# Pairs of tiles in the MLP passes, biases in three bfloat16 rows, and an edge attention that clears its PSUM bank two ahead

## The reference, cut to what matters

```
x = x + gnn(ln(x)) + mix(ln(x))      # two graph attention layers and an MLP; a curvature mixer
x = x + routed_ffn(ln(x))            # an MLP whose result is scaled by a weight per node
x = x + gcn(ln(x)) + transformer(ln(x))   # graph convolution; 4 layers of linear attention and MLP
x = x + experts(ln(x))               # 4 small MLPs, gated by a graph attention over 65,536 edges

# one graph attention layer: for each edge, 8 heads of 32
e = sum(q[dst] * k[src]) / sqrt(32);  m = segment_max(e, dst);  a = exp(e - m[dst])
z = segment_sum(a, dst);  agg = segment_sum(v[src] * a, dst) / z
# one MLP: 256 -> 1024 -> 256
y = act(x @ w1 + b1) @ w2 + b2
```

## Time and profile before

| | us |
|---|---|
| median of 3 runs (lowest, highest) | 8246.72 (8228.94, 8250.25) |
| the profiled execution | 8267.04 |
| its span from first to last instruction | 8265.3 |
| PE busy, share | 5754.8, 70% |
| DVE busy, share | 4931.1, 60% |
| POOL busy, share | 4726.3, 57% |
| ACT busy, share | 2389.2, 29% |
| granted TensorE clock, mean | 0.79 of full |

### The profile page before, as it was taken

One profiled execution on the slowest core, in us unless ns is written; L12 is line 12 of the kernel. 1 busy time (PEld: TensorE's weight loads), 2 busy tenths in 40 slices (PEclk: granted clock), 3 DMA queues, 4 the chain that ended last, 5 costly groups with the idle time before them and its releaser, 6 DMA issues. The chain is left out here.

```text
span 8265.3 us, 113872 instructions
## 1 busy us (share of the span) xinstructions
PE 5754.8 (70%) x30502; PEld 4427.0 (54%) x30502; DVE 4931.1 (60%) x10093; ACT 2389.2 (29%) x6859; POOL 4726.3 (57%) x4113
## 2 busy tenths in 40 slices
PE   3443588888875888888685865957868858677743
PEld 1333455555544555555464653856756747556632
DVE  9367477787765777878676165363354453411157
ACT  0243044444440444444422311211212212122211
POOL 0777577777732777777304656565565565167730
PEclk9766777777777777877797977978979979788865
DMA  2000476666633766666400122322313324222201
GB/s 36 4 1 4 116 180 174 172 175 174 171 106 99 181 173 172 178 174 174 123 5 17 29 78 53 86 73 72 95 46 93 95 52 100 57 53 46 46 4 50
DMA packets 686241, 772.10 MB, mean 93 GB/s; under 512 B 469870, under 2 KB 514659, under 8 KB 684593
## 3 DMA queue, kind: packets, MB, share of 16 engines
q0 software_dynamic: 557488, 618.01, 30.6%
q1 hardware_dynamic: 128232, 147.68, 6.2%
HBM read 720.03 MB, written 42.63 MB: 92 GB/s over the span
## 5 line engine op out<-in xcount | busy, mean ns | idle before, releaser
L1492 POOL DMA_INDIRECT arena<-kv_rows,visit_src x1664 | 2051.7, 1233 | 872.0 <-issue 473.3
L1978 POOL DMA_INDIRECT arena<-piece_rows,visit_src x832 | 1034.5, 1243 | 799.9 <-PE ps L2035 571.8
L1645 PE MATMUL ps<-arena,w 125*125 x4992 | 917.1, 350 | 53.9 <-DVE stage L1532 39.1
L1645 PEld LDWEIGHTS ps<-arena,w 125*125 125x125 bf16 x4992 | 816.6, 176 | 184.8 <-issue 155.8
L1744 ACT CAST ps<-cat 125x265 bf16 x1664 | 637.7, 383 | 931.8 <-PE ps L1684 604.5
L1684 PE MATMUL ps<-h,cat 125*125 125x265 f32 x1664 | 700.2, 545 | 218.6 <-ACT ps L1744 194.8
L724 POOL DMA_INDIRECT sorted<-arena,cat x512 | 576.8, 1127 | 477.1 <-PEq L84 276.9
L637 PE MATMUL ps<-ht,w 128*128 128x125 f32 x6400 | 834.4, 284 | 12.0 <-DVE ht L674 7.9
L603 ACT ACTIVATE h<-ps,vec 128x125 f32<-128x125 f32 x1600 | 463.2, 366 | 1251.2 <-PE ps L637 1251.0
L637 PEld LDWEIGHTS ps<-ht,w 128*128 128x128 f32 x6400 | 768.0, 196 | 61.2 <-issue 55.6
L628 PE MATMUL ps<-ident,stage 125*128 125x125 f32 x1200 | 257.8, 300 | 753.8 <-ACT stage L588 655.2
(11 more groups left out here) (558 smaller groups left out, 9690.5 us busy)
## 6 DMA issues: line engine op xcount, KB each, us to landing
w<-rel SPq DMA_DIRECT2D x104, 488.3 KB
arena<-kv_rows,visit_src POOLq DMA_INDIRECT x1664, 5.6
arena<-rel SPq DMA_DIRECT2D x34, 512.0 KB
arena<-piece_rows,visit_src POOLq DMA_INDIRECT x832
kv_rows<-h SPq DMA_DIRECT2D x50, 250.0 KB
x_kept<-arena POOLq DMA_DIRECT2D x3, 3125.0 KB
arena<-tab,visit_src POOLq DMA_INDIRECT x537
by_low<-steer POOLq DMA_INDIRECT x512, 2.1
```

Of the source, the lines that this page charges most:

```text
L1492: nc.gpsimd.indirect_dma_start(ring[k % RG][:, j, :], None, d.kv, bass.IndirectOffsetOnAxis(g.srcv[:, v:v + 1], 0)).then_inc(got[k % RG], 16)
L1645: ins = nc.tensor.matmul(psQ[n][:, j * D:(j + 1) * D], ohT[b % 4][:, e:e + P], q[:, bass.ds(at[2 * n + j], D)], start=(m == 0), stop=(m == 2))
L1978: nc.gpsimd.indirect_dma_start(self.rows[v % (self.RG * GG)], None, self.d.pieces, bass.IndirectOffsetOnAxis(g.srcv[:, v:v + 1], 0)).then_ ...
```

## The change

- **MLP passes** (`mlp`): they go through a new `pair_pass`, two tiles at a time, so that a matmul of the hidden layer has 250 moving columns; the results of both tiles share a PSUM bank. The passes of the experts stay as they are (`expert_mlp`).
- **Biases** of these passes and of the mixer's output pass: DVE splits the row once into three bfloat16 parts (`split_bias`), and PE adds it by one bfloat16 matmul over three rows.
- **Curvature mixer**: the rescale is cut off from `attend`; the order is rescale, scale_rows of the next tile, attend, keep.
- **Edge attention**: the bank two windows on is cleared, and a visit waits for the clearing of two visits before it; the rescale stands between the halves of the product; one set of weights in SBUF, doubled by batch, serves both uses; the factor lies in another bank and no longer waits for `shift` and `turn_back`; ACT makes it before the weights.
- Some weights of 32 columns move to make room.

The diff, cut to its core:

```diff
-            step(V.tensor_scalar(wn[:, 0:VC], w, 1.0, None, ALU.add))
+            step(V.tensor_scalar(wn[:, 0:VC], w, 2.0, None, ALU.add))
...
-                    if bias:
+                    if bias and hidden:
                         ins = nc.tensor.matmul(ps[u], g.ones[0:1, 0:P], home.brow[0:1, :], start=False, stop=True)
+                    elif bias:
+                        this(pe, s["bias"], 0)
+                        ins = nc.tensor.matmul(ps[u], g.ones_b[0:3, 0:P], g.bias_b, start=False, stop=True)
...
             fetch(0, 0)
+            if bias and not hidden:
+                split_bias(nc, g, Steps(dve, s["step"])).then_inc(s["bias"], 2)
...
+def split_bias(nc, g, step):
+
+    V, (hi, rest, mid) = nc.vector, g.bias_parts
+    mine = g.ident[0:3, 0:3]
+    step(V.tensor_copy(hi, g.brow[:, :]))
+    step(V.tensor_tensor(rest, g.brow[:, :], hi, ALU.subtract))
+    step(V.tensor_copy(mid, rest))
+    step(V.tensor_tensor(rest, rest, mid, ALU.subtract))
+    step(V.tensor_scalar(rest, rest, mine[:, 2:3], None, ALU.mult))
+    step(V.scalar_tensor_tensor(rest, mid, mine[:, 1:2], rest, ALU.mult, ALU.add))
+    return V.scalar_tensor_tensor(g.bias_b, hi, mine[:, 0:1], rest, ALU.mult, ALU.add)
...
+def pair_pass(nc, g, src, H, func, finish, ready, scale=None, shift=None, affine=None, side=None, weave=None):
...
+            put(0)
+            all_here(act)
+            for i, (t, n) in enumerate(pairs):
+                for j in range(nj):
+                    if j % 2 == 0:
+                        act.wait_ge(s["up"], i * nj // 2 + j // 2 + 1)
+                        if i and not j:
+                            act.wait_ge(s["down"], i)
+                    ins = nc.scalar.activation(h1[j][:, 0:n * P], up(j)[:, 0:n * P], func, bias=g.vec[:, j:j + 1])
+                    if j % 2:
+                        ins.then_inc(s["act"], 1)
+                    if j == 1 and i + 1 < len(pairs):
+                        put(i + 1)
...
+            turn(0)
+            all_here(pe)
+            for i, (t, n) in enumerate(pairs):
+                pe.wait_ge(s["fetched"], i + 1)
+                for j in range(nj):
+                    if i and j % 2 == 0:
+                        pe.wait_ge(s["act"], (i - 1) * nj // 2 + j // 2 + 1)
+                    for k in range(2):
+                        ins = nc.tensor.matmul(up(j)[:, 0:n * P], g.w1[:, k * H + j * 128:k * H + (j + 1) * 128], hT[:, k, 0:n * P],
+                                               start=(k == 0), stop=(k == 1))
+                    if j % 2:
+                        ins.then_inc(s["up"], 1)
+                    if j == nj // 2 - 1 or j == nj - 1:
+                        places(n)
+                if i + 1 < len(pairs):
+                    turn(i + 1)
+                if i:
+                    pe.wait_ge(s["kept"], t)
+                for u in range(n):
+                    for j in range(nj):
+                        if u == 0 and j % 2 == 0:
+                            pe.wait_ge(s["act"], i * nj // 2 + j // 2 + 1)
+                        nc.tensor.matmul(down[u], h1[j][:, u * P:(u + 1) * P], g.w2[:, j * D:(j + 1) * D], start=(j == 0), stop=False)
+                    if i == 0 and u == 0:
+                        pe.wait_ge(s["bias"], 1)
+                    ins = nc.tensor.matmul(down[u], g.ones_b[0:3, 0:P], g.bias_b, start=False, stop=True)
+                ins.then_inc(s["down"], 1)
+                places(n)
...
+            fetch(0)
+            split_bias(nc, g, Steps(dve, s["step"])).then_inc(s["bias"], 1)
+            for i, (t, n) in enumerate(pairs):
+                places(2 * n)
+                if i + 1 < len(pairs):
+                    fetch(i + 1)
+                dve.wait_ge(s["down"], i + 1)
+                for u in range(n):
+                    finish(nc.vector, t + u, u, down).then_inc(s["kept"], 1)
+                places(n)
...
                 def slot(t, u, behind, ahead, ahead2):
-                    attend(t, u)
+                    rescale(t, u)
                     if ahead:
                         scale_rows(t + 1, 1 - u)
+                    attend(t, u)
...
-    weight = g.ps[0:P, 6, 0:128]
-    weight_z = [g.ht[0:P, 512 + 128 * n:640 + 128 * n] for n in range(2)]
+    weight = [g.ht[0:P, 512 + 128 * n:640 + 128 * n] for n in range(2)]
...
-    psF = g.ps[0:P, 7, 500:508]
+    psF = g.ps[0:P, 6, 500:508]
...
-            def multiply(k):
+            def multiply(k, between=None):
...
                 for n in range(2):
+                    if n and between is not None:
+                        rescale(between)
...
-                a = weight[:, at:at + GG * HEADS].rearrange("p (j h) -> p j h", j=GG)
+                a = weight[b % 2][:, at:at + GG * HEADS].rearrange("p (j h) -> p j h", j=GG)
...
-                if n == 2 and 1 <= b <= NB:
-                    rescale(b - 1)
+                ripe = b - 1 if n == 2 and 1 <= b <= NB else None
                 if k < GROUPS:
-                    multiply(k)
+                    multiply(k, ripe)
+                elif ripe is not None:
+                    rescale(ripe)
...
             def factor_row(b):
                 pe.wait_ge(s["carried"], b + 1)
-                pe.wait_ge(s["shifted"], b + 1)
...
-                    if k or j:
-                        pe.wait_ge(s["zeroed"], k * GG + j)
+                    if k * GG + j >= 2:
+                        pe.wait_ge(s["zeroed"], k * GG + j - 1)
...
             def factors(b):
                 act.wait_ge(s["f_made"], b + 1)
-                act.wait_ge(s["turned_back"], b + 1)
...
             def weights(b):
                 act.wait_ge(s["turned_back"], b + 1)
-                if b:
-                    act.wait_ge(s["weighed"], SG * b)
-                nc.scalar.activation(weight, psA, ACT.Exp, scale=SCALE).then_inc(s["weights"], 1)
                 if b >= 2:
-                    act.wait_ge(s["z_kept"], SG * (b - 1))
-                nc.scalar.activation(weight_z[b % 2], psA, ACT.Exp, scale=SCALE).then_inc(s["weights_z"], 1)
+                    act.wait_ge(s["weighed"], SG * (b - 1))
+                nc.scalar.activation(weight[b % 2], psA, ACT.Exp, scale=SCALE).then_inc(s["weights"], 1)
...
                 if n == 1 and chained:
+                    factors(b - 1)
+                if n == 1 and chained:
                     weights(b - 1)
-                    factors(b - 1)
...
-    return [(g.vec[:, 0:b1.shape[0] // 128], b1.rearrange("(j p) -> p j", p=128)), (g.brow[:, :], b2.rearrange("(a n) -> a n", a=1))]
+    return [(g.vec[:, 0:b1.shape[0] // 128], b1.rearrange("(j p) -> p j", p=128)), (g.brow[:, :], b2.partition_broadcast(3))]
```

More of the change, by code:

```diff
@@ L1264, in scale_rows, with views, rescale @@
                     V.tensor_scalar(cat[u], psC[u], nn[u][:, 6:7], None, ALU.mult).then_inc(s["cat_ready"], 1)
-                def attend(t, u):
-                    step = Steps(dve, s["step2"], t, 8)
+                def views(u):
+                    c3 = cat[u].rearrange("p (g c) -> p g c", g=16)
+                    q, k, v = (c3[:, :, c * 32:(c + 1) * 32] for c in range(3))
+                    return c3, q, k, v, num[u].rearrange("p (g d) -> p g d", g=16), den[u].rearrange("p (g d) -> p g d", g=16)
+                def rescale(t, u):
+                    step = Steps(dve, s["step2"], t, 4)
                     this(dve, s["nn2"], t)
@@ L1651, in turn @@
                 if b:
-                    pe.wait_ge(s["factors"], b)
+                    pe.wait_ge(s["weights"], b)
                 nc.tensor.transpose(psX, score[b % 2], g.ident[0:P, 0:P]).then_inc(s["turned"], 1)
@@ L2669, in experts @@
         one.w1, one.w2, one.vec = g.w1[:, 1024 * u:1024 * (u + 1)], g.w2[:, 1024 * u:1024 * (u + 1)], g.vec[:, 8 * u:8 * (u + 1)]
-        one.brow, one.here = (g.o[0:1, 512:768], g.proj_w) if u else (g.brow[:, :], g.mlp_w)
+        one.brow, one.here = (g.o[0:1, 512:768], g.proj_w) if u else (g.brow[0:1, :], g.mlp_w)
     def weights_of(e):
@@ L2744, in experts @@
         beside = together(weights_of(e + 1), look.beside(e, homes[e] is None)) if e + 1 < EX else look.beside(e, False)
-        mlp(nc, g, xn, 512, ACT.Gelu, homes[e], None, ready=[brief[e % 2].here], side=beside, weave=look,
-            tables=None if homes[e] is not None else [(d.y_kept, half)], rows=half, home=brief[e % 2],
-            after_put=None if homes[e] is not None else look.feed_after(e))
+        expert_mlp(nc, g, xn, 512, ACT.Gelu, homes[e], half, brief[e % 2], ready=[brief[e % 2].here], side=beside, weave=look,
+                   tables=None if homes[e] is not None else [(d.y_kept, half)],
+                   after_put=None if homes[e] is not None else look.feed_after(e))
     edge_weights(nc, g, look)
```

109 lines of the change are left out of this document (88 added, 21 removed).

## The result

The changed kernel takes **8127.84 us** in the median (8119.81 to 8129.01, 4 runs), the kernel before 8248.49 (8228.94 to 8264.68): ratio 0.9853, 95% interval 0.983 to 0.9875. The forecast was 8095, its range 7945 to 8215. The profiled execution took 8126.8, its span is 8125.1.

The account below looks back on a forecast made before the run. No engine was full; DVE's loop set the attention's 27.1 us a batch, POOL's floor 2.5 below. Savings of 48 + 6 + 10 + 2 + 87 = 153 us off 8246.7 gave 8094, stated as 8095, range 7945 to 8215.

Parts of the forecast that it names:

- the new stall of 1.5 us a batch: Edge attention: gathers starting under weigh, now with two SBUF inputs, lengthen; 1.5 us a batch, bounds 0 and 4.8.
- The drains: Edge attention after the last gather: some ten groups finish without POOL, 5 us less for each layer, 10 in all.
- Rival A: Edge attention: gathers hardly disturbed, POOL's starts locking to weigh's ends; 24.9 us a batch, 7964 us; chance 0.25.
- B: Edge attention: DVE and POOL lock so that a gather is caught in every group; 28.4 us a batch, 8316 us; chance 0.11.
- C: Attention stays where it is, held by scans, ACT's stall at weights and PE's low clock; 8181 us; chance 0.17.
- D: MLPs: the pairs of tiles give nothing, attention as forecast; 8150 us; chance 0.07.
- The zeroing: Edge attention: clearing two banks ahead mostly removes PE's wait for ACT's clearing, 2.9 us a batch.
- The rescale: Edge attention: moved behind the product's first half, its 2.2 us wait a batch falls into the wait for the pick.
- The transformer MLPs: Four MLPs limited by PE: pairs of tiles and bf16 bias save 12 us each, 48 us in all.
- The first MLP: DVE's ranking work binds in its second half, so only some ten tiles gain: 6 us saved.
- the routed one: Routed MLP: 12 us but for the cover of POOL's last scatter; at most 10, taken as 10.
- The curvature mixer: Reordered DVE work saves about 25 us there, but POOL's scatters end the stage: taken as 0, bounds -2 and +5.

Follow-up runs that it names:

- e1: Changed kernel with weigh reading its factors from PSUM again, the weights' part undone: 7936.79 us, ratio 0.9609 to the kernel before.
- e5: e1 with one edit, weigh reading the copy of the weights in SBUF: 8161.93 us, ratio 0.989 to the kernel before.
- e4: Changed kernel with the six MLPs in single tiles and float32 bias as before: 8196.42 us, ratio 0.9921 to the kernel before.
- e7: e1 with the clearing only one bank ahead again: 8206.57 us, ratio 0.9942 to the kernel before.
- e6: e1 with the rescale back at the head of its group, ahead of the product's first half: 7937.58 us, ratio 0.9615 to the kernel before.
- e3: Changed kernel with the clearing only one bank ahead again: 8141.4 us, ratio 0.986 to the kernel before.
- e10: Kernel before with only the clearing two banks ahead, on a chip 16% slower for every program: 9443.63 us, ratio 0.9872 to the kernel before.

## Why the prediction was right, and where it was off

**The mechanism of the attention was right, its price too low, and part of the total is luck.** POOL became the limit by gathers that begin under weigh, and the signs came as named: mean over 1.30 (1.366), long gathers exactly under weigh, POOL's wait for weigh and the rescale's wait gone, DVE waiting for gathers. The failed term is the new stall of 1.5 us a batch. It measured 16 x 1.366 - 16 x 1.239 = 2.0, which puts the floor at 26.7 and not 26.1. The count of gathers was right (2.9 by chance, 3.1 measured), the 0.55 us for each too (0.53), 1.65 us a batch together. What was left out is that `hot` runs into weigh without a gap: a gather that begins under `hot`, long by 0.23 us in e1, must wait for both and is long by 0.46. With more gathers beginning there (51, before 8) this adds 0.7 a batch, and the other long gathers take 0.3 less.

So the attention gave 58 us and not 87. From first to last gather it gave 18 where 77 were put down: the floor was 0.6 us too low in each of 104 batches, 62 us. (At the stage's start the sum itself was short: from 25.0 to 26.2 are 1.2 us for each of ten batches and not 0.8; 1.7 were measured.) The drains gave 40 where 10 were put down. Nothing in the prediction foresaw these 30 us, nor the 10 of the curvature mixer and some 14 more in and around the transformer's MLPs; they stand against most of what the attention's middle and the first and the routed MLP fell short. That the time lies near the forecast is luck to that extent.

**Rival A did not come, but was priced well.** With the gathers undisturbed it put 7964 and 24.9 us a batch; e1, which takes the disturbance away, took 7937 and 24.8. B did not come: 2.0 us a batch is less than the 3.1 from which it decides. The nearest to it is e5 with a mean of 1.391, 27.1 us a batch. C is refuted by e1, D by e4. (D's 8150 is not what the sum gives: without the 64 us of the pairs the same forecast is 8158.)

**The zeroing.** Its wait was taken as gone; 29.1 of 85.7 us are left. That it is last in the ring was right: e7 to e1 is 270 us. 231 of them lie between first and last gather, 2.2 us a batch, as the prediction's 27.1 and rival A's 24.9 have it; 34 lie in the drains. ACT's stall before the weights was said to stay at 126.9 us in 800; before `factors` and `weights` together it is 73.5 now. That it does not carry the period shows in e1, with 89.9 us of it and 24.8 us a batch.

**The rescale** was counted as gone into the wait for the pick. Its wait is gone, and e6 shows that this gained nothing: with the clearing two ahead the sum that it waits for comes early enough.

**The transformer MLPs** gave 14.1 us each, not 12: of the standstill of 0.18 us, which was kept whole in the bias, about 0.1 is left (0.24 to 0.25 us where 0.32 was put). The passes around them gave another 7 us in sum, where 2 were expected; of what, no run tells. **The first MLP** gave 2.8 and not 6, **the routed one** 5.3 and not 10: 7 us lie between the start of POOL's last scatter and the next stage's first, and they were left out of the cover. The next stage's first scatter came 12.5 us after the last one before; 12.5 less 7.1 is 5.4, and that is all that could be gained there.

**The curvature mixer** was taken as 0, with bounds of -2 and +5 us, and gained 9.8. That the stage ends on POOL was right. That POOL's part could shrink, since its scatters are disturbed by the very instructions that were moved, was seen, but only its loss was bounded wide.

**The sum** in the spans was 153 against 140.2 measured. The other 20 us of the miss of 33 come from the reference: the profiled execution of before lay 18.5 us above its median, that of the changed kernel 1.0 below its own. In which stage those 18.5 us lie is not known. If they lie in the attention's loop, as the scatter of e4 suggests, its gain by the medians is nearer to 40 than to 58 us.

## What to carry to other kernels

When an edit removes the wait that limits a loop, price what every other edit does to the engine that is next: here one operand's place cost 11 us where POOL had slack and 225 us where it had none. Where POOL issues indirect DMAs beside DVE and is near its limit, try giving DVE's instructions one PSUM input rather than two in SBUF, and count instructions that follow each other without a gap as one. Where a stage ended on POOL's last DMA here, the next stage's first came some 7 us after that one's start (6.7 and 7.1).

## What the runs showed of the hardware that was not expected

- A long gather that begins under a DVE instruction with two SBUF inputs ends 1.08 us after that instruction, whatever its start: twice in the rows shown, and 1.08 to 1.09 us in all 89 long gathers that begin under weigh from 1400 to 2200 in the changed kernel. The longest of all took 2.90 us.
- TensorE's granted clock in the attention rose from 0.76 to 0.89 with the change, to 0.90 in e1 and 0.81 in e7, while PE was less busy in each of them than before (70%, 75% and 80% for 83%; part of that is the clock itself, since the same matmuls take less time at a higher one). PE's short waits for the clearing are a tempting reason (175 before, 38 now, 157 in e7), and between e1 and e7 only the clearing differs. But e3 has 141 of them, 71.1 us, at 0.87. So their number alone does not set the clock, and the cause stays open.
- The attention's loop can settle at different rates when its code is the same: 480 and 474 gathers in 800 us in the changed kernel and in e4, and 24.8 against 25.9 us a batch and more in e6 and e10, on two chips.
